# Recurrence of a gated network: one 128x64 multiplication for two gates from a block-diagonal state, with the state written twice by VectorE

## The reference

```python
def step(carry, xs):
    h, c = carry
    xi_t, xf_t, xg_t, xo_t = xs
    i_t = sigmoid(xi_t + h @ V_i)
    f_t = sigmoid(xf_t + h @ V_f)
    g_t = tanh(xg_t + h @ V_c)
    o_t = sigmoid(xo_t + h @ V_o)
    c_new = h * c + i_t * g_t
    h_new = o_t * tanh(c_new)
    return ((h_new, c_new), h_new)
```

## Time and profile before

| | |
|---|---|
| median of 3 runs | 1088.16 us (1087.66 to 1088.91) |
| the profiled execution | 1085.05 us |
| its span, first to last instruction | 1083.2 us |
| the recurrence in it, first state multiplication to last state | 192.7 to 630.9 us |
| mean granted TensorE clock, whole span | 0.738 |
| granted TensorE clock in the recurrence | 0.50 |
| one step | 1.70 us |

### The profile page before, as it was taken

How to read it: one execution, slowest core, us unless ns; L and a number is a source line. 1 busy time by engine, 2 the same in 40 slices (tenths; PEclk the granted TensorE clock), 3 DMA queues, 4 the chain that set the end, 5 groups by cost and what they waited for, 6 DMA issues and landing times.

```text
span 1083.2 us, 18938 instructions
## 1 busy us (share of the span) xinstructions
PE 800.7 (74%) x6224; PEld 584.8 (54%) x6224; DVE 648.6 (60%) x1576; ACT 603.9 (56%) x1660; POOL 442.2 (41%) x343
## 2 busy tenths in 40 slices
PE   5787876666666666666666467877876999999996
PEld 2565664555555555555555434665753666556664
DVE  4999972355535535433333339999925766656775
ACT  2575763333335545433333326666746888878884
POOL 0688775000000000000000006788845888868885
PEclk8899987555555555555555558889986999999998
DMA  9500000000000200000000000000000010010000
GB/s 224 128 1 0 0 1 1 1 1 1 1 1 17 118 3 1 1 1 1 1 1 1 1 0 2 1 1 0 0 1 1 2 67 4 3 70 2 2 2 20
DMA packets 5852, 18.41 MB, mean 17 GB/s; under 512 B 1093, under 2 KB 2822, under 8 KB 5254
## 3 DMA queue, kind: packets, MB, share of 16 engines
q1 hardware_dynamic: 5478, 17.21, 5.5%
q10 hardware_dynamic: 288, 0.13, 0.1%
HBM read 9.47 MB, written 0.52 MB: 9 GB/s over the span
## 4 chain that ended last, share of the span: by engine, by line
POOL 35%; PE 20%; issue 19%; ACT 12%; DVE 12%; DVEq 1%; POOLq 1%; DMA 0%; SPq 0%; ACTq 0%
POOL zw L790 19%; POOL hid L754 15%; PE bank L464 9%; DVE cell L1040 5%; PE bank L466 5%; ACT tcell L696 5%; ACT scan_io L692 5%; DVE hr L1046 4%; PE bank L304 2%; PE bank L271 1%; POOL xs L747 1%; PE bank L283 1%; PE bank L337 1%; POOLq L789 1%; DVEq L1039 0%
## 5 line engine op out<-in xcount | busy, mean ns | idle before, releaser
L754 POOL TENSOR_TENSOR hid<-smat,shi 128x512 f16<-128x512 f32 x144 | 219.2, 1547 | 560.0 <-ACT smat L598 559.9
L790 POOL TENSOR_TENSOR zw<-hid,zw 128x512 f16<-128x512 f32 x176 | 204.3, 1161 | 49.9 <-ACT zw L723 33.2
L464 PE MATMUL bank<-hr,lv 64*64 64x8 f32 x512 | 96.9, 261 | 166.5 <-DVE hr L1046 166.5
L464 PEld LDWEIGHTS bank<-hr,lv 64*64 64x64 f32 x512 | 72.6, 200 | 213.1 <-DVE hr L1046 212.9
L1145 DVE SCALAR_TENSOR_TENSOR hid<-bank,wsc,st 128x512 f32<-128x512 f32 x176 | 132.0, 751 | 76.6 <-ACT st L727 70.2
L692 ACT ACTIVATE scan_io<-bank 64x16 f32<-64x16 f32 x256 | 49.2, 192 | 210.4 <-PE bank L466 210.2
L879 DVE TENSOR_TENSOR st<-tent,tentx 128x768 f32<-128x768 f32 x96 | 155.9, 1689 | 1.7
L1040 DVE TENSOR_TENSOR_SCAN cell<-scan_io 64x32 f32<-64x32 f32 x256 | 55.4, 216 | 160.2 <-ACT scan_io L692 160.1
L507 PE MATMUL bank<-st,wh 128*128 128x512 f16 x352 | 136.9, 389 | 11.9 <-POOL st L783 5.4
L727 ACT ACTIVATE st<-bank,wsc 128x512 f32<-128x512 f32 x176 | 121.0, 688 | 36.3 <-PE bank L508 18.7
L508 PE MATMUL bank<-st,wl 128*128 128x512 f16 x352 | 136.8, 389 | 0.0
(11 more groups left out here) (149 smaller groups left out, 1274.1 us busy)
## 6 DMA issues: line engine op xcount, KB each, us to landing
w13s<-w SPq DMA_DIRECT2D x8, 704.0 KB, 16.6
w2f<-w SPq DMA_DIRECT2D x4, 384.0 KB, 26.6
w13s<-wh SPq DMA_DIRECT2D x2, 704.0 KB, 3.4
w13s<-wl SPq DMA_DIRECT2D x2, 704.0 KB, 4.6
wh<-w13s SPq DMA_DIRECT2D x2, 704.0 KB, 4.3
wl<-w13s SPq DMA_DIRECT2D x2, 704.0 KB, 5.5
w2f<-w2p SPq DMA_DIRECT2D x2, 384.0 KB, 5.1
w2p<-w2f SPq DMA_DIRECT2D x2, 384.0 KB, 5.2
```

Of the source, the lines that this page charges most:

```text
L464: nc.tensor.matmul(both[:, 0, t, :], lv[:, C:2 * C], prev, start=False, stop=True, skip_group_check=True)
L754: nc.gpsimd.tensor_tensor(slo[:, place(p, g), :, :], smat[:, g % RING, :, :], shi[:, place(p, g), :, :], ALU.subtract).then_inc(s(c + "s_l ...
L790: nc.gpsimd.tensor_tensor(hl[:, u % MR, :], hid[:, u % MR, :], hh[:, u % MR, :], ALU.subtract)\
```

## The change

Input gate and candidate come from one multiplication. The weight tile `lv` is now 128x64: the input gate's V on partitions 0 to 63, the candidate's V on partitions 64 to 127 (the output gate's goes to a tile of its own, `lvo`). The state is kept block-diagonal: for each step 128 partitions x 2 blocks x 8 images, with h in block 0 on partitions 0 to 63, h again in block 1 on partitions 64 to 127, and zeros elsewhere. One multiplication by these 16 columns gives both gates in the layout that L692 reads. `hr` lies in `smat` now. VectorE writes the two copies of h with two products, the one on partitions 64 to 127 first. The output gate is a Sigmoid on ScalarE (`og`) in place of a Tanh, so that h = og x tcell is a plain product, and not 2h; factors of one half in other places go. The weights `lv` come in three DMAs in place of one. A filler loop that ran zero times is deleted.

```diff
-        lv = sb("lv", [C, 192])
+        lv = sb("lv", [P, C])
+        lvo = sb("lvo", [C, C])
-        hr = sb("hr", [C, 2 * W, B])
-        tog = sb("tog", [C, B])
+        og = sb("og", [C, B])
+        hr = spare[:, 0:4 * W * B].rearrange("p (n k b) -> p n k b", k=2, b=B)
...
-            sp.dma_start(lv[:, :], lstm_v).then_inc(s("ld_lstm"), 16)
+            sp.dma_start(lv[0:C, :], lstm_v[:, C:2 * C]).then_inc(s("ld_lstm"), 16)
+            sp.dma_start(lv[C:2 * C, :], lstm_v[:, 0:C]).then_inc(s("ld_lstm"), 16)
+            sp.dma_start(lvo[:, :], lstm_v[:, 2 * C:3 * C]).then_inc(s("ld_lstm"), 16)
...
-                pe.wait_ge(s("l_h"), n + 1)
-                prev = hr[:, (n - 1) % (2 * W), :]
-                both = bank[r % 2][0:C, 0:256].rearrange("p (k b t) -> p k t b", k=2, t=W)
+                pe.wait_ge(s("l_h"), 2 * n + 1)
+                prev = hr[:, (n - 1) % (2 * W), :, :]
+                both = bank[r % 2][0:C, 0:256].rearrange("p (kb t) -> p t kb", t=W)
-                nc.tensor.matmul(both[:, 0, t, :], lv[:, C:2 * C], prev, start=False, stop=True,
-                                 skip_group_check=True)
-                nc.tensor.matmul(both[:, 1, t, :], lv[:, 0:C], prev, start=False, stop=True,
+                nc.tensor.matmul(both[:, t, :], lv[:, :], prev.rearrange("p k b -> p (k b)"), start=False, stop=True,
                                  skip_group_check=True).then_inc(s("l_gi"), 1)
-                nc.tensor.matmul(go, lv[:, 2 * C:3 * C], prev, start=False, stop=True,
+                nc.tensor.matmul(go, lvo[:, :], prev[0:C, 0, :], start=False, stop=True,
                                  skip_group_check=True).then_inc(s("l_o"), 1)
...
-                                     hr[:, r % 2 * W:r % 2 * W + W, BQ * hf:BQ * hf + BQ].rearrange("p t b -> p b t"),
-                                     ACT.Copy, scale=0.5).then_inc(s("l_up"), 1)
+                                     hr[0:C, r % 2 * W:r % 2 * W + W, 0, BQ * hf:BQ * hf + BQ].rearrange("p t b -> p b t"),
+                                     ACT.Copy).then_inc(s("l_up"), 1)
...
-                nc.scalar.activation(tog[:, :], go, ACT.Tanh).then_inc(s("l_oact"), 1)
+                nc.scalar.activation(og[:, :], go, ACT.Sigmoid).then_inc(s("l_oact"), 1)
...
-            for part, factor in ((lu[:, :, C:3 * C], 0.5), (lb[:, C:3 * C], 0.5),
-                                 (lv[:, 0:C], 0.5), (lv[:, C:3 * C], 0.25)):
-                nc.gpsimd.tensor_scalar(part, part, factor, None, ALU.mult).then_inc(s("l_scaled"), 1)
+            for part in (lu[:, :, C:2 * C], lb[:, C:2 * C], lv[0:C, :]):
+                nc.gpsimd.tensor_scalar(part, part, 0.5, None, ALU.mult).then_inc(s("l_scaled"), 1)
...
-            nc.vector.memset(hr[:, 2 * W - 1, :], 0.0).then_inc(s("l_h"), 1)
+            nc.vector.memset(hr, 0.0).then_inc(s("l_h"), 1)
...
-                nc.vector.scalar_tensor_tensor(out=hr[:, n % (2 * W), :], in0=tog[:, :], scalar=1.0, in1=tcell[:, :],
-                                               op0=ALU.add, op1=ALU.mult).then_inc(s("l_h"), 1)
+                for k in (1, 0):
+                    nc.vector.tensor_tensor(hr[k * C:k * C + C, n % (2 * W), k, :], og[:, :], tcell[:, :], ALU.mult)\
+                        .then_inc(s("l_h"), 1)
                 if n < STEPS - 1:
-                    dve.wait_ge(s("l_h"), n + 2)
-                    nc.vector.scalar_tensor_tensor(out=scan_io[:, 0, :, 3], in0=hr[:, n % (2 * W), :], scalar=0.5,
-                                                   in1=cell[:, :, 3], op0=ALU.mult, op1=ALU.mult)\
-                        .then_inc(s("l_hc"), 1)
+                    dve.wait_ge(s("l_h"), 2 * n + 3)
+                    nc.vector.tensor_tensor(scan_io[:, 0, :, 3], hr[0:C, n % (2 * W), 0, :], cell[:, :, 3],
+                                            ALU.mult).then_inc(s("l_hc"), 1)
```

More of the change, by code:

```diff
@@ L48 @@
 CHUNK = 256
-FILL = 0
 E = 8
@@ L424, in _ @@
             norm(1, [("c0_res", 1 + BQ)])
-            pe.wait_ge(s("ld_lstm"), 16 * 3)
+            pe.wait_ge(s("ld_lstm"), 16 * 5)
             pe.wait_ge(s("n1_xn"), 2)
-            pe.wait_ge(s("l_scaled"), 4)
+            pe.wait_ge(s("l_scaled"), 3)
             pe.wait_ge(s("l_init"), 4)
@@ L475, in _ @@
                     gates_x(r + 1, t - 3)
-                for _ in range(FILL):
-                    nc.tensor.matmul(bank[7][:, :], samp[0][:, 0, 0:128], samp[0][:, 0, 0:512],
-                                     start=True, stop=True)
             pe.wait_ge(s("ld_late"), 32)
@@ L701, in _ @@
                         high_part(2 * PAIRK * part + n - SPLIT[part])
-            act.wait_ge(s("l_h"), STEPS + 1)
+            act.wait_ge(s("l_h"), 2 * STEPS + 1)
             for hf in range(2):
@@ L766, in _ @@
             conv(0)
-            gp.wait_ge(s("ld_lstm"), 48)
-            for part, factor in ((lu[:, :, C:3 * C], 0.5), (lb[:, C:3 * C], 0.5),
-                                 (lv[:, 0:C], 0.5), (lv[:, C:3 * C], 0.25)):
-                nc.gpsimd.tensor_scalar(part, part, factor, None, ALU.mult).then_inc(s("l_scaled"), 1)
+            gp.wait_ge(s("ld_lstm"), 80)
+            for part in (lu[:, :, C:2 * C], lb[:, C:2 * C], lv[0:C, :]):
+                nc.gpsimd.tensor_scalar(part, part, 0.5, None, ALU.mult).then_inc(s("l_scaled"), 1)
             conv(1)
```

## The result

| | before | after |
|---|---|---|
| median, 20 runs each | 1086.51 us (1081.16 to 1088.91) | 1089.22 us |
| ratio | | 1.0028, 95% interval 1.0015 to 1.0041 |
| span of the profiled execution | 1083.2 us | 1084.1 us |
| first to last scan of the recurrence (255 steps) | 435.1 us | 436.9 us |

The median of the kernel before is over 20 runs here, the three of above among them. One run of the kernel after took 1162.61 us at a granted clock of 0.635, where the others had 0.736 to 0.746, and is left out of the ratio. By the ratio the change costs 0.28%, 3 us (1.6 to 4.5): it is slower, where I had forecast 6 us faster.

The account below looks back on a forecast made before the run. A chain through TensorE, VectorE and ScalarE, 1.70 us a step, was taken to bound the recurrence. -0.200 and +0.172 over 256 steps gave -7.2 us, with +1.0 for a table load -6.2: 1082.0 us, range 1058 to 1094.

Parts of the forecast that it names:

- Part 2: VectorE, state products: the second starts after the first ends, state ready at 0.324 instead of 0.157, +0.17 us a step.
- Part 1: TensorE, gate multiplications: two become one, 0.39 us in place of 0.59, -0.20 us a step.
- A: VectorE, the forecast itself: second product held until the first ends; own range 1072.5 to 1092 us; chance 0.62.
- Part 3: Side jobs on VectorE and ScalarE in the recurrence: they stay covered beside the chain and cost nothing.
- Part 4: One-time work: ring clearing, DMAs and scalings cost nothing; one more function-table load in the first step, +1.0 us.
- rival D: ScalarE: no table holds both Sigmoid and Tanh, so each step loads twice, about 1740 us; chance 0.03.
- The sum: Whole kernel: -7.2 us from the steps and +1.0 for the table, together -6.2, 1082.0 us; nothing else changes.
- B: VectorE: the two state products overlap, -0.115 us a step, 1059.8 us; chance 0.17.
- C: TensorE: tile form's change paid before the gates, +0.042 us a step, 1100 us; chance 0.18, including similar chain costs.

Follow-up runs that it names:

- the dummy Tanh: Kernel before plus one dummy Tanh on ScalarE ahead of the recurrence, so the function table loads in idle time; ratio 0.9982.
- only one product: Kernel after without the product that writes the state's copy on partitions 64 to 127; 1038.27 us, ratio 0.957.
- the single multiplication from the weights' side: Kernel before with a 64x128 weight tile giving both gates in one multiplication, state unchanged, two tanh on ScalarE; 1137.06 us, ratio 1.0458.
- VectorE's part alone: Kernel before plus a first product writing a copy to partitions 64 to 127 of an unread tile, three multiplications kept; 1137.65 us, ratio 1.047.
- with Tanh: Kernel after with the output gate by Tanh again, and the factors of a half and a quarter back; ratio 0.9999.

## Why the prediction was wrong

**The step that failed** is Part 2, the price of the second product, by its size. The prediction worked it out as 0.152 + 0.02 + 0.152 in place of 0.157, which is +0.167, and then set +0.172 into its sum, for which it gives no reason. The runs show +0.193 (one product against two) and, by the rows, 0.159 a product with 0.03 between them. The choice between the two readings was right: the held one, and not the overlap. Both sizes were too small, and both stood in the rows. The product's length I took from a line through two larger ones and set under the fused form's 0.157, though that was the nearest row. The gap of 0.02 was a wrong reading of the earlier trace rows: of the 0.60 for both copies the first has 0.29, but the second only 0.28, as a narrow window of the same timeline shows:

```profile
642.75 0.28 DVE L862 COPY pad<-xn 64x256 f32<-64x256 f32 x1
```

The first ends at 642.43 + 0.29 = 642.72, so the gap is 0.03 there too. With 0.157 and 0.03 the price is +0.19, and the sum would have been (-0.20 + 0.19) x 256 + 1.0 = -1.6 us: no change that can be measured. Of the 7.2 us that the regular steps were to give, the term took back 0.021 x 256 = 5.4.

**Part 1** was right: -0.20 predicted, 0.63 to 0.43 in the timelines, -0.193 from the run without the second product (the other 0.007 x 256 = 1.8 us). The pair of 16 columns spans 0.39, as worked out, and the 128 rows cost nothing that shows.

So the net was a difference of two large terms, -0.20 and +0.17, each known to 0.02 or so, and it was used as if it were known. Measured, the regular step is the same, 1.700 us. The result (+3 us) lies inside the range of A, in its slower part, to which I gave 0.05 of 0.62. It isn't there for the reason that the bound names, a step longer by 0.01: the trace has +1.0 from the table and +0.9 from long steps. (The +0.159 under the other end of A's range is worked out nowhere.) By these terms no change was the likeliest outcome, not faster.

**Part 3** held: the side jobs are covered (even with one product, 0.19 us lie between the end of L1007 and the scan). Only once, where several small jobs for the scale factors stand on VectorE, is the scan 0.05 late; in another step TensorE comes 0.06 late from its own job for them. The output gate stayed beside the chain: L691 ends at 408.30 and L693 starts at 408.36.

**Part 4**: the table load was +1.0 as taken, and one only; rival D falls. The Trainium skill (ScalarE: Activation LUTs, "Table sets: the hidden batching unit") lists tanh in the sigmoid's set too, and the trace agrees: after the load at the first Sigmoid there is none in the other 255 steps.

**The sum** said that nothing else changes, and that was a second miss: the long steps, +0.9 us. They go with VectorE's stream, which is 256 instructions longer. Where it has its old length (the kernel before, with and without the dummy Tanh, only one product, and the single multiplication from the weights' side) VectorE is 0.35 late in steps 30, 138, 162 and 212. Where it has the second product (the kernel after and its runs with two products on VectorE) VectorE is late by 0.2 to 0.4 in steps 7, 44, 62, 81, 119, 177, 198 and 241 instead. VectorE's part alone on the kernel before, in which no other engine's stream was changed, has its long steps in just these eight, so they come with VectorE's stream and with nothing else of the change. Of the two views, the first is step 162 of the kernel before; the second is step 62 of the run with VectorE's part alone, and it looks like step 62 of the kernel after, shown above:

```profile
470.49 0.16 DVE L1046 SCALAR_TENSOR_TENSOR hr<-tog,tcell 64x8 f32<-64x8 f32 x1 [0.70 <-ACT tcell L696]
```

```profile
313.31 0.16 DVE L1049 SCALAR_TENSOR_TENSOR hr<-tog,tcell 64x8 f32<-64x8 f32 x1 [0.23 <-issue]
```

In a regular step VectorE sits idle for 0.35 before the first instruction, in place of 0.70, and for 0.01 before the second, in place of 0.23. Where GpSimd writes the second copy, VectorE is late in its four old steps, and GpSimd 0.3 late in steps 57, 121, 185 and 249, each 64 behind the one before. What the engine does in that time no view shows; it stays open.

**Rivals B and C**: B is refuted: the two products of the change don't overlap, and the run with both on the same partitions shows what decides it; its price was right (+0.085 predicted, 1.583 - 1.507 = 0.076 measured). C is refuted: the multiplication starts 0.06 behind the second product although the one before it had another form, and its result comes 0.43 after its start, where 0.42 was forecast and C asks for 0.07 more in all. The Trainium skill (VectorE: DVE Perf Modes, "Two Vector instructions with no wait between them") says that a held instruction starts only when every earlier Vector instruction has finished, and that an output in another quadrant of 32 partitions holds it. The traces of the kernel after and of both products on the same partitions agree: 0.19 between starts with different output partitions, 0.084 with the same ones.

## What to carry to other kernels

Where a chain through several engines sets the time, an instruction added on one engine must be priced with its full length and gap if it writes other partitions than its neighbour (0.19 us here; on ScalarE, where the next reads other partitions, 0.20), and with less than half of that if it doesn't (0.08). The gap must be read at its full resolution, from a window that holds one instruction alone: 0.01 us a step was 2.6 us here. Before a multiplication is saved by a second copy of its operand, ask which engine makes the copy: on an engine that is idle and runs beside, the trade wins (0.053 us a step here), in a row on the same one it is nil. And when a forecast is the difference of two terms of 0.2 us that are each known to a tenth, the honest forecast is no change.

## What the runs showed of the hardware

- Of two tanh on ScalarE that read different halves of the PSUM partitions the second starts 0.20 us after the first (0.18 long), 0.02 after its end; the next, on the same half as the second, starts 0.10 behind it, in its midst (the multiplication from the weights' side). That two instructions read one bank doesn't keep them apart: here both read the same bank on the same partitions, and the second starts 0.18 before the first ends (kernel before):

```profile
59.87 0.66 ACT L594 ACTIVATE shi<-bank 128x512 f16<-128x512 f32 x1
60.35 0.67 ACT L598 ACTIVATE smat<-bank 128x512 f32<-128x512 f32 x1
```

- An fp32 weight load of 128 columns takes 0.308 us and one of 64 columns 0.200 at the granted clock of 0.50, 1.2 GHz; one multiplication with 128 weight columns (0.59 for its pair) is as long as two with 64.
- TensorE starts 0.15 us after the end of a GpSimd product by the rows, and 0.06 after one of VectorE (GpSimd's spans are rough, and TensorE waits for two semaphores in the first case).
- A GpSimd product of 64x8 takes 0.198 us, against VectorE's 0.159.
- A second VectorE product on other partitions starts 0.03 us after the end of the first where that one signals (kernel after, and with Tanh), and 0.01 where it doesn't (VectorE's part alone); on the same partitions it starts 0.084 after the first's start.
- VectorE starts an instruction 0.2 to 0.4 us late with no wait to explain it at places that stay the same while its stream has the same number of instructions: four in the 256 steps before, eight after.
